# Two-layer block on one core: the convolution of layer 1 moved from TensorE to VectorE, one broadcast comparison, and the last tile finished by halves

## What is computed

```python
x_ssm, gate = split(x @ W_in + b_in)
xc = conv_general_dilated(x_ssm.T, conv_w, padding=[(3, 0)], feature_group_count=128) + conv_b  # 4 taps, each feature by itself
x_conv = silu(xc.T)
B, C = split(x_conv @ W_x + b_x)
h = exp(-exp(A_log)) * h + x_conv * B        # 16 states a feature, step by step along the tokens
y = sum_n(C * h) + D * x_conv
s = (y * silu(gate)) @ W_out + b_out
```

## Time and profile before

| | us |
|---|---|
| three executions | 575.06, 577.42, 578.22 (median 577.42) |
| the profiled execution | 576.23 |
| its span | 574.4 |
| TensorE / VectorE / GpSimd / ScalarE busy | 479.3 / 406.1 / 381.6 / 291.5 |
| mean granted clock of TensorE | 0.952 of full speed |

### The profile page before, as it was taken

One profiled execution on the slowest core, in us unless ns is written; L12 is line 12 of the kernel. 1 busy time (PEld: TensorE's weight loads), 2 busy tenths in 40 slices (PEclk: granted clock), 3 DMA queues, 4 the chain that ended last, 5 costly groups with the idle time before them and its releaser, 6 DMA issues.

```text
span 574.4 us, 6068 instructions
## 1 busy us (share of the span) xinstructions
PE 479.3 (83%) x1915; PEld 281.6 (49%) x1915; DVE 406.1 (71%) x638; ACT 291.5 (51%) x468; POOL 381.6 (66%) x372
## 2 busy tenths in 40 slices
PE   0796879897999799989999799979997999685672
PEld 0574645544665456555655365545654565232220
DVE  2273134869686988877796889796869777859793
ACT  2663636663675556463747464646755544332300
POOL 1552542978586868876877869686878688644553
PEclk9987979999999999998999999999999999887985
DMA  8300000000000010001000100001000000000000
GB/s 315 150 19 3 1 19 1 1 1 18 0 2 0 1 55 1 1 2 55 2 0 2 41 15 0 0 2 37 1 1 2 18 1 1 0 19 1 5 14 18
DMA packets 5794, 11.83 MB, mean 21 GB/s; under 512 B 896, under 2 KB 1664, under 8 KB 5504
## 3 DMA queue, kind: packets, MB, share of 16 engines
q1 hardware_dynamic: 4608, 9.47, 4.5%
q10 hardware_dynamic: 1152, 1.93, 1.0%
HBM read 9.30 MB, written 2.10 MB: 20 GB/s over the span
## 4 chain that ended last, share of the span: by engine, by line
PE 58%; DVE 15%; ACT 13%; issue 6%; POOL 5%; DMA 1%; SPq 0%; POOLq 0%; DVEq 0%; ACTq 0%
PE bank0a L866 19%; PE bank1a L946 6%; PE ybank L1009 5%; PE bank1d L984 5%; PE bank0a L977 5%; DVE hs L1275 4%; PE xbank L995 3%; DVE xbank L1263 3%; DVE plain L1174 2%; PE bank1d L971 2%; PE bank1a L931 2%; DVE beats L1237 2%; ACT plain L587 2%; PE bank0d L839 2%; POOL hs L495 2%
## 5 line engine op out<-in xcount | busy, mean ns | idle before, releaser
L495 POOL TENSOR_TENSOR hs<-hs,Ct 128x512 f32<-128x512 f32 x128 | 168.6, 1319 | 27.7 <-DVE hs L1275 22.6
L1263 DVE TENSOR_TENSOR xbank<-xbank,Bt 128x512 f32<-128x512 f32 x128 | 88.2, 689 | 32.0 <-PE xbank L995 31.6
L995 PE MATMUL xbank<-xpair,spr 128*128 128x512 f32 x128 | 75.8, 594 | 33.6 <-DVE hs L1275 33.6
L468 POOL TENSOR_TENSOR hidAl<-plain,hidAh 128x512 fp32r<-128x512 f32 x48 | 62.7, 1306 | 43.6 <-ACT hidAh L588 36.3
L587 ACT ACTIVATE plain<-bank0a,col 128x512 f32<-128x512 f32 x64 | 44.1, 689 | 89.2 <-PE bank0a L866 89.1
L468 POOL TENSOR_TENSOR hidBl<-plain,hidBh 128x512 fp32r<-128x512 f32 x48 | 62.5, 1301 | 39.3 <-ACT hidBh L588 27.7
L1275 DVE TENSOR_TENSOR_SCAN hs<-decay,carry,xbank 128x512 f32<-128x512 f32 x64 | 81.8, 1279 | 7.4
L1275 DVE TENSOR_TENSOR_SCAN hs<-decay,xbank 128x512 f32<-128x512 f32 x64 | 78.0, 1219 | 4.9
L866 PE MATMUL bank0a<-hidBh,hTh 128*128 128x512 f32 x128 | 57.2, 447 | 1.6 <-ACT hidAh L588 1.6
L866 PE MATMUL bank0a<-hidAh,hTh 128*128 128x512 f32 x128 | 56.4, 441 | 2.2 <-ACT hidBh L588 2.2
L995 PEld LDWEIGHTS xbank<-xpair,spr 128*128 128x128 f32 x128 | 24.5, 191 | 68.7 <-DVE hs L1275 45.0
(11 more groups left out here) (170 smaller groups left out, 981.4 us busy)
## 6 DMA issues: line engine op xcount, KB each, us to landing
xt<-x_tok SPq DMA_DIRECT2D x8, 256.0 KB, 2.6
xr<-x_feat SPq DMA_DIRECT2D x8, 256.0 KB, 7.6
out<-xr SPq DMA_DIRECT2D x8, 256.0 KB, 2.0
fh<-h_w SPq DMA_DIRECT2D x1, 1024.0 KB, 10.9
hs<-h_w SPq DMA_DIRECT2D x1, 1024.0 KB, 12.4
lw<-l_w ACTq DMA_DIRECT2D x1, 640.0 KB, 6.7
g<-spread ACTq DMA_DIRECT2D x1, 512.0 KB, 6.2
Bt<-w_in SPq DMA_DIRECT2D x1, 512.0 KB, 8.5
```

The source lines that it names most:

```text
L468: pool.tensor_tensor(low[:, m, :], plain[:, k % NPLAIN, :], high[:, m, :].bitcast(F32), ALU.subtract).then_inc(hidden_low, 1)
L495: pool.tensor_tensor(h, h, Ct[:, hs_(u)], ALU.mult).then_inc(p_ready, 1)
L995: pe.matmul(xbank[i % 2][:], spr[:, at, :], xpair[:, half, hs_(u)], start=True, stop=True).then_inc(xs_full, 1)
L1263: dve.tensor_tensor(xbank[i % 2][:], xbank[i % 2][:], Bt[:, hs_(u)], ALU.mult).then_inc(xb_ready, 1)
```

## The change

What it does, part by part:

- TensorE's four-tap convolution is gone, with w_conv, its load conv_rows and GpSimd's multiplication. TensorE makes one projection ("conv") into bank1a in slot 4. ScalarE copies it into xc with the scale of tap 3 (start_taps, slot 4) and, in even tiles, keeps the last three columns. VectorE adds the three other taps from the bank (convolve, slot 5, behind the scan), each step waiting for the one before, then the edge: one 128x3 addition in even tiles, three operations on 1 to 3 columns in odd ones. ScalarE's SiLU then works on xc in place.
- On TensorE the gate's projection moves from slot 5 to slot 6, and B behind it: gate, B, C follow each other behind the second h1 tile. The spread of a tile's first step moves from the start of slot 7 to behind the score.
- VectorE: residual_l0 moves behind the scan of slot 0; low_x from slot 6 to slot 7; the four comparisons with the other half become one tensor_tensor over 4x512 columns with both inputs broadcast; the output product of tile 6 moves from slot 15 of period 7 to slot 0 of period 8, GpSimd's addition with it.
- End: the last scan, its weighting, its gather, the gate's product, the output projection, the output product, the addition (now on VectorE) and the store go by halves of 256 columns.

```diff
@@ ScalarE
+            def start_taps(t):
+                if t >= 2:
+                    act.wait_ge(yg_ready, t - 1)
+                act.wait_ge(l1_act_full, done(L1_ACT, ("conv", t)))
+                last = act.activation(xc[:, hs_(t)], bank1a[:], ACT.Copy, scale=scale("conv_w", TAPS - 1))
+                if t % 2 == 0:
+                    last = act.activation(z_last[:], bank1a[:, HALF - TAPS + 1:], ACT.Copy)
+                last.then_inc(taps_started, 1)
             def convolved(t):
...
-                take1(("conv", t), xc[:, hs_(t)], ACT.Silu, bias=b_conv[:, 0:1])
+                act.wait_ge(conv_step, conv_steps(t + 1))
+                act.activation(xc[:, hs_(t)], xc[:, hs_(t)], ACT.Silu, bias=b_conv[:, 0:1]).then_inc(l1_act_done, 1)
@@ TensorE, slot
-                    if u_next is not None:
+                    if u_next is not None and k_next > 0:
                         spread_x(u_next, k_next)
...
                         if s == 4:
-                            convolve(n, (3, 2, 1, 0))
-                        elif s == 5:
-                            project("gate", n, W_IN[:, P:2 * P])
-                        elif s == 6:
-                            project_x("B", n, W_B)
+                            project("conv", n, W_IN[:, 0:P])
                     if v is not None and 5 <= s < 5 + KT:
                         hidden("h1", v, s - 5)
                     if n is not None:
                         if s == 6:
+                            project("gate", n, W_IN[:, P:2 * P])
+                            project_x("B", n, W_B)
                             project_x("C", n, W_C)
                         elif s == 7:
                             project("score", n, W_R)
                         elif s == 8:
                             score_column(n)
+                    if u_next is not None and k_next == 0:
+                        spread_x(u_next, k_next)
@@ VectorE
+            def convolve(t):
+                dve.wait_ge(taps_started, t + 1)
+                at = conv_steps(t)
+                for i in range(1, TAPS):
+                    if i > 1:
+                        dve.wait_ge(conv_step, at + i - 1)
+                    dve.scalar_tensor_tensor(xc[:, t % 2 * HALF + i:t % 2 * HALF + HALF], bank1a[:, 0:HALF - i],
+                                             scale("conv_w", TAPS - 1 - i), xc[:, t % 2 * HALF + i:t % 2 * HALF + HALF],
+                                             ALU.mult, ALU.add).then_inc(conv_step, 1)
...
+            def compare_other(u):
...
+                dve.tensor_tensor(beats[:, CPH:], row.broadcast_to([P, CPH, HALF]), s_i.broadcast_to([P, CPH, HALF]),
+                                  ALU.is_le if u % 2 else ALU.is_lt).then_inc(beats_ready, CPH)
...
+            def finish_last():
...
+                for part in range(2):
+                    dve.tensor_tensor(yg[:, quarter(part)], ybank[:, half_of(part)], gate[:, quarter(part)],
+                                      ALU.mult).then_inc(yg_ready, 1)
...
+                    dve.scalar_tensor_tensor(g1[:, quarter(part)], (bank1d, bank1a)[part][:, half_of(part)], scale("b_out"),
+                                             g1[:, quarter(part)], ALU.add, ALU.mult).then_inc(l1_dve_done, 1)
...
+                    dve.tensor_tensor(x_half, g1[:, quarter(part)], x_half, ALU.add).then_inc(o_ready, 1)
@@ VectorE, slot
-                    if s == 0:
-                        residual_l0(n)
-                    elif s == 2:
+                    if s == 2:
                         stats_l1(n)
-                    elif s == 6:
+                    elif s == 7:
                         low_x(n)
                 if u is not None:
                     scan(u, k)
+                if n is not None:
+                    if s == 0:
+                        residual_l0(n)
+                    elif s == 5:
+                        convolve(n)
```

More of the change, by code:

```diff
@@ L417, in _ @@
             load_feat(7)
-            for t in range(4, UNITS):
+            for t in range(4, UNITS - 1):
                 store(t)
+            for h in range(2):
+                sp.wait_ge(o_ready, UNITS + h)
+                sp.dma_start(out[BATCH - 1][:, quarter(h)], xr[:, (BATCH - 1) % 2, quarter(h)]).then_inc(stored[3], 16)
             for i in range(4):
-                sp.wait_ge(stored[i], UNITS // 4 * 16)
+                sp.wait_ge(stored[i], UNITS // 4 * 16 + (16 if i == 3 else 0))
         @block.gpsimd
@@ L490, in weigh_states @@
                 pool.wait_ge(xs_done, i + 1)
+                if i == LAST:
+                    for part in range(2):
+                        pool.wait_ge(xs_done, i + 1 + part)
+                        pool.tensor_tensor(h[:, half_of(part)], h[:, half_of(part)], Ct[:, quarter(part)],
+                                           ALU.mult).then_inc(p_ready, 1)
+                    return
                 if u % 2 == 0:
@@ L553, in _ @@
             act.dma_start(grow[:], gamma_row).then_inc(params, 16)
-            for dst, src in ((raw_spr, spread), (lw[:], l1_w), (gat[:], gather), (tri, before_mask), (w2l[:], w2_l1),
-                             (gate[:, 0:TAPS * P], conv_rows)):
+            for dst, src in ((raw_spr, spread), (lw[:], l1_w), (gat[:], gather), (tri, before_mask), (w2l[:], w2_l1)):
                 act.dma_start(dst, src).then_inc(l1_params, 16)
@@ L1010, in gather_y, with project_last @@
                                   start=False, stop=(quad == NGRP // QUAD - 1)).then_inc(y_full, 1)
+                    if last_quad:
+                        rows = slice((QUAD - 1) * P // QUAD, P)
+                        for part in range(2):
+                            pe.wait_ge(p_ready, LAST + 1 + part)
+                            pe.matmul(ybank[rows, half_of(part)], gat[:, at:at + P // QUAD],
+                                      hs[:, LAST % NSTATES, half_of(part)], start=False, stop=(part == 1)).then_inc(y_full, 1)
+                def project_last():
+                    open1d(("out", UNITS - 1))
+                    pe.wait_ge(l1_act_done, done(L1_ACT, ("score_col", UNITS - 1)))
+                    for part in range(2):
+                        pe.wait_ge(yg_ready, UNITS + part)
+                        pe.matmul((bank1d, bank1a)[part][:, half_of(part)], W_OUT, yg[:, quarter(part)], start=True,
+                                  stop=True).then_inc(l1_dve_full, 1)
                 def project_out(t):
@@ L1235, in compare @@
                 j = c - u % 2 * CPH
-                if not 0 <= j < CPH:
-                    dve.tensor_scalar(bt, row, s_i, None, ALU.is_le if j < 0 else ALU.is_lt).then_inc(beats_ready, 1)
-                    return
                 if r == 0:
@@ L1321, in slot @@
                         mod_update(t)
[L1322 to L1323 removed]
+                    if t == UNITS - 1 and s == 0:
+                        output(e)
                 if n is not None:
```

107 lines of the change are left out of this document (66 added, 41 removed).

## The result

The changed kernel takes 588.5 us (median of 4, 587.0 to 590.4) against 576.2 for the kernel before (median of 4): ratio 1.0205, 95% interval 1.0173 to 1.0238. It is slower by 12 us, and 0.5 us above the range.

A forecast was written before the change was run, and what follows sets the result against it. VectorE was taken to pace slots 2 to 5, TensorE slots 5 to 1. Terms -1.5 + 4.8 + 3.4 + 1.3 - 0.8 - 3.6 = +3.6 on 576.2 gave 579.8, as median 581.0; range 569 to 588.

The forecast's parts named there:

- The tempting 23 us: Eight tiles: TensorE relieved of some 2.9 us each by losing the convolution; named as tempting, not taken as the gain.
- +0.8 a tile: Middle tiles 1 to 6: later C and first spread, partly returned by the shorter comparison; ends +0.3 and +1.3, total +4.8.
- the clock: Middle tiles: TensorE's clock falls in three of six at 1.7 us each, less the one before: +3.4, bounds 0 and +10.
- Rival B: Whole kernel: stalls as forecast, but the clock stays at 2.4 GHz: +0.2, 577.6 us; chance 0.22.
- Rival E: Clock falls in every tile and stays low past C: 590 us; chance 0.05.
- Wrong sign: tile 0: First tile: no scans delay the taps, C comes at about 93, the spread later: -1.5 us (0 to -2.5).
- the gain at the end, -3.6 forecast: End of the kernel: last scan through final addition by halves, -3.6 us (ends -2 and -4.5).
- the output move: Tile 7: tile 6's output product behind the comparison waits for nothing, first rank at 545.3 instead of 546.0: -0.8 us.
- the residual product behind the scan: Start of each tile: scan fills part of VectorE's idle 3.93 us; counted at nothing, 1.2 us a tile if cover went.
- tile 7, +1.3 forecast: Last tile: no h1 tiles; convolution, gate, B, C and spread chain +1.7, less 0.4 at the comparison: +1.3 us.
- Rival C: Middle tiles break even because the slot 10 comparison lets VectorE catch up, clock kept: 572 us; chance 0.24.
- Rival D: Six middle tiles: relief kept, slots 2 to 5 run ahead and C comes 2.5 us sooner: 561 us; chance 0.05.

The follow-up runs named there:

- d1: b3 plus three chained VectorE products of 509 to 511 columns a tile in slot 5, on dead data nobody reads: 568.7 us, ratio 0.9857.
- a3: The changed kernel with four comparisons in place of the one broadcast comparison: 587.6 us, ratio 1.0182.
- b1: The kernel before with only the broadcast comparison in place of four: 575.2 us, ratio 0.9987.
- a2: The changed kernel with the third h1 tile placed between B's projection and C's on TensorE: 583.8 us, ratio 1.0135.
- d2: b3 plus the changed kernel's TensorE order alone (gate, B, C in a row, late first spread, low_x in slot 7), convolution on TensorE: 595.2 us.
- b3: The kernel before with only the end by halves, the moved output of tile 6 and the residual product behind the scan: 568.1 us, ratio 0.9852.
- f2: The kernel before with only tile 6's output product and its addition moved behind tile 7's comparisons: 573.1 us, ratio 0.9958.
- d4: b3 with only the first spread moved behind the column scores and low_x into slot 7; gate and B left in place: 571.7 us, ratio 0.9908.
- e1: a3 with the gate projected and taken before the convolution, and ScalarE taking B ahead of the first h1 tile: 574.6 us, ratio 0.9956.
- f1: e1 with the first spread back at the head of slot 7 and low_x in slot 6: 572.6 us, ratio 0.9944.
- a1: The changed kernel with ScalarE taking B's projection directly behind the gate's, ahead of the first h1 tile: 591.3 us, ratio 1.0258.

## Where the prediction was right, and where it was wrong

The mechanism of the forecast was the right one, and its sign; its sizes were too small, and the time fell outside the range. The sum was 10.6 us short (579.8 against the profiled 590.4; by the medians 7.5, 581.0 against 588.5): 4.9 in the middle tiles, 2.7 in tile 0, 2.8 in tile 7 and the end, 0.2 ahead of tile 0. The step that failed most is one: I priced TensorE's lower clock in the middle tiles alone and too low there, and gave tiles 0 and 7 none.

**Right in the middle tile.** By the distance from the residual product, SiLU came 2.0 us later (2.1 forecast), C 0.9 (1.0), the gate's product 1.2 (1.4); the waits were 1.00, 0.89 and 2.03 (1, 1.1, 2.1); the comparison 2.79, and 2.27 in odd tiles (2.28 to 3.6). The tempting 23 us were rightly refused. Counting VectorE's added work for nothing but its place in the chain was right too: d1 shows it.

**Too small: +0.8 a tile.** Tiles 2 and 4 have +1.27 and +1.28, at my upper end. I let the shorter comparison pay a part back. It paid nothing: VectorE returned 0.8 us in slot 10, but GpSimd, held out for the comparison's length, released the D matmul late. I had bounded the comparison by one GpSimd operation that VectorE waits for, and never asked the reverse, what GpSimd waits for. a3 puts it at 0.25 us in such a tile, b1 at 0.6 in the old order; the other 1.0 I take for C's delay, handed on undiminished. The Trainium skill (SBUF — State Buffer, SBUF: two separate sides) says that a VectorE instruction with two inputs in SBUF and a GpSimd operation that reads SBUF exclude each other for the whole instruction. By that rule I should have counted up to the comparison's whole length for GpSimd; the 2.25 us copy agrees with it.

**Too small: the clock.** I let it fall in three of six tiles. It fell in four, in two of them twice. Six tiles at the clean price would be 6 x 1.27 = 7.6 us longer; 13.1 were measured, and the 5.5 between them I put down to the clock, where I had 3.4. It is an estimate, as no odd middle tile of the changed kernel kept its clock; in a2 tiles 1, 2, 4 and 5 did, and were 0.6 to 1.2 us longer than before, the odd ones no more than 0.2 above the even. Rival B (the clock stays) is refuted; its own sum also kept the one fall of the kernel before, and without it would have been -1.5 in place of +0.2. From 66 us on, the clock is at 1.2 GHz for some 45 us before and some 83 after. Rival E (every tile) was wrong for the changed kernel: tiles 2 and 4 kept the full clock. In d2, where TensorE also has the taps to do, it fell in each of the first seven. The Trainium skill (TensorE: Matmul & The Clock Gate, What's actually happening) lets the clock follow how busy the array has lately been; read as I read it, all six middle tiles would have fallen, and tiles 2 and 4 don't agree. What decides it is not settled here.

**Wrong sign: tile 0.** I took -1.5 since C comes earlier, and it did (93.39 against 94.67; 93 forecast). But tile 0 is +1.24. The step that failed is that I priced the clock in the middle tiles alone: behind C it is at 1.2 GHz from 93 to 100 us, and C itself takes 2.07 us instead of 1.12.

**Too large: the gain at the end, -3.6 forecast, -2.2 measured.** From the start of the last scan to the end of the span it is 10.0 us in the changed kernel and 12.2 before (9.8 in b3, 12.3 in f2). The scan and GpSimd's product by halves came as forecast, 1.5 and 2.3 us behind that start. The last gather ended at 3.6 where I had 2.9, and the output projections at 6.3 where I had 4.6: at 1.2 GHz they took 1.19 and 1.06 us. The last addition ended at 7.35, not 6.2.

**About right: the output move.** It brought the first rank from 55.7 to 54.9 us behind the residual product in f2 (-0.8, as forecast), and f2's stretch from that product to the end is 83.05 against 84.13, so -1.1.

**Put at nothing: the residual product behind the scan.** TensorE's own work hides it in the middle tiles, whose length is the same in b3 as before. It does not in tile 7: there the convolution's first matmul comes 11.5 us behind the residual product in the changed kernel and 12.7 before. That is the 1.2 us which I had named as the gain if the cover went.

**Too small: tile 7, +1.3 forecast.** The stretch is 0.3 us shorter than before. With -2.2 for the end, -1.1 for the output move and -1.3 for the residual product, tile 7 itself costs 4.3 us; the split is an estimate, as two of its terms come from other runs or from one matmul's place. I had placed gate, B and C in a chain whose order and waits were right (3.81, 0.78, 0.84) and gave each matmul pair 1.1 us; B, C and the score ran at 1.2 GHz, 2.08 us each. It is the step that failed in tile 0: no clock outside the middle.

**What I did not see at all.** I treated the order of TensorE as a companion of the convolution. d2 shows that the order alone costs 27 us over b3 with the convolution left in place, 24 of them the place of gate and B (d2 against d4). Moving the convolution, given that order, gives 8.5 us back (a3 against d2). e1 shows that VectorE's convolution needs no such order. Yet even in f1, the best order tried, it is some 5 us slower than b3, which leaves it on TensorE.

Rival C, the gain side, had the comparison as its place: b1 and a3 show no gain there. Rival D needed slots 2 to 5 to run ahead; no middle tile of the changed kernel came under 61.8 us. Its 561 also left out the gains of the end, with which six tiles at -2.5 us would give 558.

## What to carry to other kernels

When work is moved from one engine to another, price the new order of what remains apart from the move: run the order alone. Here a bank that passes one tile at a time from TensorE to ScalarE was 24 us better with independent matmuls between its users, and what ScalarE did between two takes became TensorE's wait; moving that wait elsewhere, as a1 and a2 did, gave little or nothing. The first tile and the last, with less filler, paid their stalls and then the lower clock, so each gets its own line in the sum, with a clock of its own.

## What the runs showed of the hardware

A 128x1 copy on GpSimd took 2.25 us beneath VectorE's 128x2048 broadcast tensor_tensor, and 0.19 with no comparison beside it; in tile 7 a 128x512 product took 3.23 us there (1.27 elsewhere). The reverse is in d1: its three near-equal products with both tensor inputs in SBUF took 748, 1084 and 1532 ns in the mean. The three took 2.31 us together in tile 0, where GpSimd was idle, and 4.07 in tile 4 beside two products of GpSimd, which took 1.7 us each instead of 1.3. The convolution's taps, with one input in PSUM, took 731 to 749 ns each beside the same two products, which stayed at 1.3.

Tiles 2, 4 and 6 of the changed kernel have the same waits before gate, B and C (1.0, 0.9, 2.0 us). The granted clock fell at C in tile 6 and stayed at 2.4 GHz in the other two; in tile 6 it had also been at 1.2 GHz from 451 to 454 us, ahead of the gate. A fall lasted 3 to 7 us in the middle tiles. A projection of 512 columns in two matmuls took 1.12 us at 2.4 GHz and 2.08 at 1.2.
